# One matmul stream cut into small pieces: convolution and transposes interleaved on TensorE, with seven landing slots ahead of it

## What is computed

```python
x = x + conv3x3_int8(group_norm(x, 16 groups), weight, bias)   # per-tensor scales: max|.| over all of x
x = x + spectral(group_norm(x, 16 groups), R)                  # rfft2, keep 32 x 16 modes, mix channels, irfft2
```

## Time and profile before

| | |
|---|---|
| time, median of 3 runs (range) | 3774.03 us (3768.83 to 3782.59) |
| the profiled execution's own time, and its span | 3779.11 us, 3777.3 us |
| mean granted clock of TensorE | 0.909 |
| first stage, about 10 to 765 us | VectorE 576 of 715 us busy, DMA 362 GB/s |
| second stage, 790 to 2427 us | TensorE 1567, VectorE 1542, ScalarE 1360 of 1637 us busy, DMA 328 GB/s |
| last stage, 2515 to 3777 us | VectorE 1061 of 1262 us busy, DMA 419 GB/s |

### The profile page before, as it was taken

How to read it: one execution, slowest core, us unless ns; L and a number is a source line. 1 busy time by engine, 2 the same in 40 slices (tenths; PEclk the granted TensorE clock), 3 DMA queues, 4 the chain that set the end, 5 groups by cost and what they waited for, 6 DMA issues and landing times.

```text
span 3777.3 us, 81588 instructions
## 1 busy us (share of the span) xinstructions
PE 3106.2 (82%) x33145; PEld 1541.2 (41%) x33145; DVE 3256.8 (86%) x3336; ACT 2350.9 (62%) x3443; POOL 823.0 (22%) x1040
## 2 busy tenths in 40 slices
PE   5565566569999999999999999878888888888886
PEld 1111111136666666666666666543222222222222
DVE  5878878799999998999999998669888888888887
ACT  5777777768888787878888888643333333333332
POOL 0000000035455454545455454300000000000000
PEclk7767666689999999999999999989999999999998
DMA  9999999999999999999999999749999999999998
GB/s 359 366 359 356 357 361 365 357 250 356 336 319 347 306 354 295 352 306 345 324 332 334 317 346 301 279 170 427 427 427 427 427 427 427 427 423 422 421 421 370
DMA packets 342540, 1352.55 MB, mean 358 GB/s; under 512 B 45792, under 2 KB 47040, under 8 KB 243808
## 3 DMA queue, kind: packets, MB, share of 16 engines
q1 hardware_dynamic: 223104, 811.13, 60.0%
q0 software_dynamic: 82272, 268.58, 19.8%
q10 hardware_dynamic: 36864, 268.45, 16.9%
HBM read 811.10 MB, written 536.87 MB: 357 GB/s over the span
## 4 chain that ended last, share of the span: by engine, by line
DMA 39%; DVE 34%; PE 14%; issue 6%; ACT 5%; SPq 1%; POOL 0%; DVEq 0%; ACTq 0%
DMA out<-ring 19%; DVE ring L561 12%; DMA ring<-in_x 11%; DMA ring<-x_scratch 9%; DVE area L543 6%; ACT area L312 4%; PE ps L721 4%; DVE area L538 4%; PE ps L683 4%; DVE area L547 3%; DVE ring L658 3%; PE ps L732 2%; DVE area L556 2%; PE ps L742 1%; DVE mixb L566 1%
## 5 line engine op out<-in xcount | busy, mean ns | idle before, releaser
L288 POOL DMA_DIRECT2D x_scratch<-ring x1024 | 817.0, 804 | 1596.9 <-DVE ring L561 1574.1
L868 PE MATMUL ps<-x,gj_s 128*128 128x512 bf16 x3072 | 773.6, 406 | 217.2 <-DVE ring L658 216.2
L721 PE MATMUL ps<-area,wq 128*32 128x512 bf16 x12264 | 764.8, 383 | 51.0 <-DVE ring L561 33.7
L658 DVE TENSOR_TENSOR ring<-ps,ring 128x1024 f32<-128x1024 f32 x512 | 603.0, 1219 | 162.5 <-DMA ring<-x_scratch 159.2
L561 DVE SCALAR_TENSOR_TENSOR ring<-ps,sc,ring 128x1024 f32<-128x1024 f32 x512 | 634.2, 1278 | 19.7 <-PE ps L721 12.6
L683 PE MATMUL ps<-ring,negm_s 128*32 128x512 f32 x2048 | 391.4, 905 | 313.4 <-DMA ring<-in_x 313.4
L337 ACT ACTIVATE area<-ps 128x512 f32<-128x512 f32 x1024 | 553.2, 595 | 116.2 <-PE ps L732 115.2
L868 PEld LDWEIGHTS ps<-x,gj_s 128*128 128x128 bf16 x3072 | 294.8, 103 | 773.9 <-DVE ring L658 442.8
L732 PE MATMUL ps<-id_s,ring 128*128 128x128 f32 x4096 | 561.3, 280 | 16.2 <-ACT area L337 14.1
L466 DVE TENSOR_REDUCE stat<-area 128x1 f32<-128x4096 f32 x128 | 559.1, 4410 | 7.1 <-ACT area L312 7.0
L344 ACT ACTIVATE area<-ring,qtab 128x2048 bf16<-128x2048 f32 x256 | 513.1, 2004 | 0.0
(11 more groups left out here) (123 smaller groups left out, 2006.3 us busy)
## 6 DMA issues: line engine op xcount, KB each, us to landing
ring<-in_x SPq DMA_DIRECT2D x256, 1024.0 KB, 7.9
ring<-in_x SPq DMA_DIRECT2D x1024, 256.0 KB, 6.9
x_scratch<-ring POOLq DMA_DIRECT2D x1024, 256.0 KB, 6.6
ring<-x_scratch SPq DMA_DIRECT2D x256, 1024.0 KB, 11.7
out<-ring ACTq DMA_DIRECT2D x256, 1024.0 KB, 25.3
ring<-in_rt SPq DMA_DIRECT2D x1, 4096.0 KB, 15.2
area<-in_gj SPq DMA_DIRECT2D x1, 768.0 KB, 4.7
eh_s<-in_eh SPq DMA_DIRECT2D x1, 128.0 KB, 2.0
```

The costliest lines, as they stand in the source:

```text
L288: pool.dma_start(x1_rows[b, m, r], xslot(t % SL)[32 * r:32 * r + 32, :].rearrange("p (g w) -> p g w", g=4)).then_inc(s_x_out[t % SL], 16)
L658: nc.vector.tensor_tensor(half, ps[0][:, hj * 2 * HW:(hj + 1) * 2 * HW], half, ALU.add).then_inc(s_add, 1)
L721: last = mm(ps[0][32 * cg:32 * cg + 32, HW * g:HW * g + HW], wq[:, (3 * a + dw) * C:(3 * a + dw + 1) * C], src[:, 1 + dw:1 + dw + HW], sta ...
L868: last = mm(bank(j), gj_s[:, (j * 3 + v) * 128:(j * 3 + v + 1) * 128], (z12, z12, z13)[v][:, k % 2], start=(v == 0), stop=(v == 2))
```

## The change

Three things are changed, all in the first two stages.

The first stage gets seven landing slots in place of four; slots 4 to 6 are the buffers `vbuf`, `mixb` and `x2`, which only later stages use. The first loads of the second stage wait for the last group that used their slot.

`rows_copied` moves from VectorE to ScalarE, in two places of its loop, and the rest of the small work of an image is put later: the copy of the height transform from j = 5 to 6, `dc_first` from 6 to 7, `sums` from 6 to 8, `spread` from 7 to 9, `variance` from 7 to 11, `root` from 8 to 12, `spectra` from 9 to 12, `spectrum` from 9 to 14. The loops run to T + 20 instead of T + 15.

On TensorE, `conv` and `turn_x1` are cut into a group of four matmuls (one g and dw) and a single transpose. `conv_and_turn(i-2, i-4, h)` issues six groups of four, and behind each of them one transpose, behind the third and the sixth two. The same instructions are issued as before, in another order, with the same semaphores.

```diff
+        NGS = 7
+
         def gslot(k):
-            return ring[:, k * FT:(k + 1) * FT]
+            return ring[:, k * FT:(k + 1) * FT] if k < 4 else (vbuf, mixb, x2)[k - 4][:, 0:FT]
...
-                if n >= 4:
-                    sp.wait_ge(s_sq, n - 3)
+                if n >= NGS:
+                    sp.wait_ge(s_sq, n - NGS + 1)
                 for c in range(GC):
-                    sp.dma_start(gslot(n % 4)[:, c * FC:(c + 1) * FC], x_chan[GC * n + c]).then_inc(s_g_in[n % 4], 16)
+                    sp.dma_start(gslot(n % NGS)[:, c * FC:(c + 1) * FC],
+                                 x_chan[GC * n + c]).then_inc(s_g_in[n % NGS], 16)
...
-                    sp.wait_ge(s_sq, NT - 3 + t // 2)
+                    sp.wait_ge(s_sq, max(n for n in range(NT) if n % NGS == t // 2) + 1)
                 load(t)
...
+            def rows_copied(b, n):
+                act.wait_ge(s_vt, 8 * b + n + 1)
+                act.activation(vt[:, :, 4 * n:4 * n + 4, :],
+                               bank(7).rearrange("p (c g k) -> p g c k", c=4, g=8), ACT.Copy).then_inc(s_vte, 1)
...
-            for i in range(T + 15):
+            for i in range(T + 20):
                 b, j = divmod(i - (TB + 5), TB)
                 small = i >= TB + 5
                 if i + 1 < T:
                     scaled(i + 1)
                 if 6 <= i and i - 6 < T and (i - 6) % 4 == 3:
                     w_copied(i - 6)
-                if small and j == 5:
+                if small and j == 6:
                     h_copied(b)
+                if small and 1 <= j < 5:
+                    rows_copied(b, 2 * j - 1)
                 if 4 <= i and i - 4 < T:
                     turned(i - 4, 0)
                     turned(i - 4, 1)
                     squared(i - 4)
+                if small and j < 4:
+                    rows_copied(b, 2 * j)
+                if 4 <= i and i - 4 < T:
                     turned(i - 4, 2)
                     turned(i - 4, 3)
-                if small and j == 8:
+                if small and j == 12:
                     root(b)
...
-            def rows_copied(b, n):
-                dve.wait_ge(s_vt, 8 * b + n + 1)
-                nc.vector.tensor_copy(vt[:, :, 4 * n:4 * n + 4, :],
-                                      bank(7).rearrange("p (c g k) -> p g c k", c=4, g=8)).then_inc(s_vte, 1)
...
-            for i in range(T + 15):
+            for i in range(T + 20):
                 b, j = divmod(i - (TB + 5), TB)
                 small = i >= TB + 5
                 if 3 <= i and i - 3 < T:
                     combine(i - 3, 0)
                     combine(i - 3, 1)
-                if small and 1 <= j < 5:
-                    rows_copied(b, 2 * j - 1)
                 if i < T:
                     quantise(i)
                 if i == T:
                     nc.vector.memset(qs[64:128, 15, :], 0.0).then_inc(s_q, 1)
-                if small and j < 4:
-                    rows_copied(b, 2 * j)
-                if small and j == 6:
+                if small and j == 8:
                     sums(b)
-                if small and j == 7:
+                if small and j == 11:
                     variance(b)
-                if small and j == 9:
+                if small and j == 14:
                     spectrum(b)
 
...
-            def conv(t, h):
-                if h == 0:
+            def conv_group(t, g, dw):
+                if dw == 0 and g == 0:
                     pe.wait_ge(s_q, t + 2)
-                if t:
-                    pe.wait_ge(s_ev, 2 * (t - 1) + h + 1)
-                for g in (2 * h, 2 * h + 1):
-                    n = 4 * (t % 4) + g
-                    above = qs[:, n - 1] if n else (qs[:, 15] if t % TB else qedge)
-                    for dw in range(3):
-                        for cg, a, src in ((1, 0, q[:, n]), (2, 1, q[:, n]), (3, 0, qs[:, n]), (0, 1, above)):
-                            last = mm(ps[0][32 * cg:32 * cg + 32, HW * g:HW * g + HW],
-                                      wq[:, (3 * a + dw) * C:(3 * a + dw + 1) * C], src[:, 1 + dw:1 + dw + HW],
-                                      start=(dw == 0), stop=(dw == 2))
-                last.then_inc(s_conv, 1)
-
-            def turn_x1(t, v):
-                if v == 0:
-                    pe.wait_ge(s_ev, 2 * t + 2)
-                if 4 * t + v >= 2:
-                    pe.wait_ge(s_te, 4 * t + v - 1)
-                for g in range(4):
-                    last = nc.tensor.transpose(bank(4 + v % 2)[:, 128 * g:128 * g + 128],
-                                               xslot(t % SL)[:, g * HW + 128 * v:g * HW + 128 * v + 128], id_s[:])
-                last.then_inc(s_t, 1)
+                if t and dw == 0 and g % 2 == 0:
+                    pe.wait_ge(s_ev, 2 * (t - 1) + g // 2 + 1)
+                n = 4 * (t % 4) + g
+                above = qs[:, n - 1] if n else (qs[:, 15] if t % TB else qedge)
+                for cg, a, src in ((1, 0, q[:, n]), (2, 1, q[:, n]), (3, 0, qs[:, n]), (0, 1, above)):
+                    last = mm(ps[0][32 * cg:32 * cg + 32, HW * g:HW * g + HW],
+                              wq[:, (3 * a + dw) * C:(3 * a + dw + 1) * C], src[:, 1 + dw:1 + dw + HW],
+                              start=(dw == 0), stop=(dw == 2))
+                if dw == 2 and g % 2:
+                    last.then_inc(s_conv, 1)
+
+            def turn_x1(t, v, g):
+                if g == 0:
+                    if v == 0:
+                        pe.wait_ge(s_ev, 2 * t + 2)
+                    if 4 * t + v >= 2:
+                        pe.wait_ge(s_te, 4 * t + v - 1)
+                last = nc.tensor.transpose(bank(4 + v % 2)[:, 128 * g:128 * g + 128],
+                                           xslot(t % SL)[:, g * HW + 128 * v:g * HW + 128 * v + 128], id_s[:])
+                if g == 3:
+                    last.then_inc(s_t, 1)
+
+            def conv_and_turn(tc, tt, h):
+                turns = [(2 * h + v, g) for v in range(2) for g in range(4)]
+                for k in range(6):
+                    if 0 <= tc < T:
+                        conv_group(tc, 2 * h + k // 3, k % 3)
+                    if 0 <= tt < T:
+                        for v, g in turns[(0, 1, 2, 4, 5, 6)[k]:(1, 2, 4, 5, 6, 8)[k]]:
+                            turn_x1(tt, v, g)
...
-            for i in range(T + 15):
+            for i in range(T + 20):
                 b, j = divmod(i - (TB + 5), TB)
                 small = i >= TB + 5
-                if 4 <= i and i - 4 < T:
-                    turn_x1(i - 4, 0)
-                    turn_x1(i - 4, 1)
-                if 2 <= i and i - 2 < T:
-                    conv(i - 2, 0)
+                conv_and_turn(i - 2, i - 4, 0)
                 if small and j < 4:
                     turn_rows(b, 2 * j)
-                if 4 <= i and i - 4 < T:
-                    turn_x1(i - 4, 2)
-                    turn_x1(i - 4, 3)
-                if 2 <= i and i - 2 < T:
-                    conv(i - 2, 1)
+                conv_and_turn(i - 2, i - 4, 1)
                 if 5 <= i and i - 5 < T:
                     along_w1(i - 5)
                 if small and j < 4:
                     turn_rows(b, 2 * j + 1)
                 if small and j == 4:
                     along_h1(b)
-                if small and j == 6:
+                if small and j == 7:
                     dc_first(b)
-                if small and j == 7:
+                if small and j == 9:
                     spread(b)
-                if small and j == 9:
+                if small and j == 12:
                     spectra(b)
```

More of the change, by code:

```diff
@@ L151, in build @@
         s_rl = sem("r_landed")
-        s_g_in = [sem(f"group_landed{k}") for k in range(4)]
+        s_g_in = [sem(f"group_landed{k}") for k in range(NGS)]
         s_cols = sem("group_column_sums_done")
@@ L311, in squares @@
                     act.wait_ge(s_max, n - 1)
-                act.activation(sqs[:, n % 2], gslot(n % 4), ACT.Square, bias=st(1, n),
+                act.activation(sqs[:, n % 2], gslot(n % NGS), ACT.Square, bias=st(1, n),
                                accum_out=st(2, n)).then_inc(s_sq, 1)
@@ L677, in column_sums @@
             def column_sums(n):
-                pe.wait_ge(s_g_in[n % 4], (n // 4 + 1) * 32)
+                pe.wait_ge(s_g_in[n % NGS], (n // NGS + 1) * 32)
                 if n >= 4:
@@ L682, in column_sums @@
                     g = j % 4
-                    last = mm(bank(n % 4)[32 * g:32 * g + 32, :], negm_s[:], gslot(n % 4)[:, j * HW:(j + 1) * HW],
+                    last = mm(bank(n % 4)[32 * g:32 * g + 32, :], negm_s[:], gslot(n % NGS)[:, j * HW:(j + 1) * HW],
                               start=(j < 4), stop=(j >= 4))
```

## The result

The changed kernel takes 4288.29 us (median of 4 runs, 4286.45 to 4292.53) against 3778.31 us of the kernel before on the same chip (3768.83 to 3788.16, 4 runs). The ratio is 1.135, 95% interval 1.132 to 1.138: 510 us slower. The forecast was 4300 us, range 4160 to 4440. The profiled execution took 4289.36 us, its span is 4287.5.

The account below looks back on a forecast made before the run. VectorE was taken to bound the second stage at 5.93 us a chunk, and TensorE at 8.50 after interleaving. 3779 + 626 (second stage) - 98 (slots) = 4307 us profiled; median 4302, say 4300, range 4160 to 4440.

Parts of the forecast that it names:

- the price of a border: Second stage, TensorE: each round trip from convolution to transposes and back costs 0.275 us; twelve make a chunk 8.50 us.
- The bet: Second stage, TensorE: a border costs the same around a single transpose as around a run, giving 8.50 us a chunk.
- 626 us longer: Second stage: 255 chunks of 8.50 us plus 84 us of small work make 2252 us, against 1626 before.
- The small work of an image: Second stage, TensorE as the bound: its own small work costs 84 us over seven images, 12 us each.
- The copies on ScalarE: Second stage: rows_copied moved off VectorE is covered in a chunk of 8.50 us, costing nothing and bringing nothing.
- Seven slots: First stage: DMA rises from 362 to 419 GB/s and binds; 124 groups save 0.79 us each, 98 us.
- the rules weighed in the forecast: TensorE: a tiling mode change drains it (8.50 us a chunk), or weight loads are pulled ahead (5.2 us).
- The rival in which everything hides: Second stage: transposes' weights load beneath the convolution, no border paid, VectorE binds at 5.93 us; 3596 us, chance 0.06.
- The break-even of that rival: Second stage: the hidden-loads rival decides at a chunk of about 6.4 us, or 0.10 us a round trip.
- the later places of the small work: Second stage: the later j are covered, VectorE's waits for TensorE's small matmuls being no longer on the path.
- The clock's rival: Second stage: TensorE's clock falls to 0.94, a chunk takes 8.9 us and the kernel 4410 us; chance 0.07.
- One reading of a row: Last stage: TensorE stands idle over a microsecond in each 4.9, its clock at 0.94.

Follow-up runs that it names:

- e4: Changed kernel with two groups of four between transposes, which come three, three and two together, six round trips a chunk instead of twelve: 3892.95 us, ratio 1.029.
- e9: Changed kernel, still interleaved, each group of four 128 x 32 matmuls made one with 128 x 128 weights (convolution computes other values): 3632.2 us, ratio 0.961.
- e11: Changed kernel with the copies of turned rows back on VectorE, small work still late: 4288.63 us, ratio 1.134.
- e1: Changed kernel with only TensorE's order undone, eight transposes of a half ahead of its six groups: 3656.3 us, ratio 0.966 against the kernel before.
- e12: Changed kernel with TensorE's block order restored and part of its small work left out (height transform 1 of 4 steps, spectra 1 of 16): 3601.55 us, ratio 0.952.
- e10: Changed kernel with the small work of an image at its old, early places, copies still on ScalarE: 4424.21 us, ratio 1.170.
- e3: Kernel before with TensorE's interleaving alone (four slots, copies on VectorE, small work at its old place): 4530.52 us, ratio 1.197.
- e5: Changed kernel, interleaved, each transpose replaced by four identity matmuls with 32 columns of the chunk as weights: 4409.24 us, ratio 1.167.
- e6: Changed kernel with each transpose replaced by four 32-column identity matmuls, in the block order of the kernel before: 4315.98 us, ratio 1.143.

## Why the prediction was right, and where it was not

The step that carries it, the price of a border read from the kernel before, held to a few per cent. I took 0.275 us for a round trip and 8.50 us a chunk; measured are 0.27 and 8.41. The bet was that a border costs a single transpose as much as a run of eight, for which the trace before had no row; e4 and the changed kernel show it at both lengths. The streams (0.216, 0.108) are unchanged, and e9 shows a chunk interleaved without its borders. The stage was forecast 626 us longer and became 611 longer.

The small work of an image was put at 12 us on TensorE. The stage has 2236.5 - 255 x 8.41 = 92 us left, 13 for each of seven ends; some 5 of the 92 stand at the stage's start, where the clock is at 0.50 from 700 to 725 us, so an end costs the 12. The copies on ScalarE were forecast to be covered: e11, 4288.63 us, shows them worth nothing.

Seven slots were forecast at 98 us, with DMA at 419 GB/s: 103 us and 421 GB/s in the trace.

Of the rules weighed in the forecast: where TensorE changes from 32-column to 128-column weights it waits, 0.33 us between starts, of which 0.216 stream. The Trainium skill's page "TensorEngine Tiling (Array Packing)", Key Properties, says that a change of tiling mode drains TensorE, and the trace agrees. Weight loads are pulled ahead too, 0.21 us in e9, but in these traces only within one shape. The Trainium skill's page "TensorE: Matmul & The Clock Gate", Step-by-step, says that loads can be pulled ahead of matmuls in flight; for the changes of shape here that did not happen.

Two statements of the forecast were wrong, neither of them a term of its sum. The rival in which everything hides was priced at 3596 us, with 11 of 16 us of each image's end saved. e1 is that state of the path and takes 3656 us: the ends cost 14 us, because I counted VectorE's waits and copies as gains and overlooked that TensorE, at 5.75 of 5.93 us, has no room for its own 12. e12 shows it. The break-even of that rival moves with it, and the chance doesn't.

And the later places of the small work I called covered, with no worth of their own. In the changed kernel they are covered, but they do something: at their old places they would have added 136 us (e10): VectorE waits ahead of its combines, TensorE then waits 48 us for these, and the clock at 1.2 GHz behind the waits costs about 90 more. A forecast of the interleaving alone by the same steps would have come out at 4385 us, with 4530 measured (e3).

The clock's rival didn't come: 0.99 over the stage. e10 shows how near it was. There the clock falls to the 0.94 that the forecast named, a chunk takes 13.8 us at half clock where it said some 14, and the kernel 4424 us where it said 4410. The forecast weighed the rival by TensorE's short pauses between groups and had no reason why the image ends would be free of longer ones. That the late places kept them free was luck.

One reading of a row was off: in the last stage TensorE stands idle (1262 - 1032.54)/256 = 0.90 us for each channel image by its records, not over a microsecond. No term hangs on it.

## What to carry to other kernels

Read TensorE from the starts of its records, not from its busy time: 2224 of 2226 us were "busy" here, and over a third of a chunk (12 x 0.27 of 8.41 us) was borders. Work of two weight shapes belongs in long runs, at 0.27 us for each round trip between 32 and 128 columns; if it must be interleaved, give both the same shape, and then weight loads hide as well. When one engine is made slower, look at what waits at the end of its turn: a small matmul there holds up the engine that should feed it next, and the pause can cost more through the clock than by its length (90 and 48 us in e10). The version to keep is e1, seven slots, the copies on ScalarE and the later small work with TensorE's order left in blocks, 3.4% faster than the kernel before.

## What the runs showed of the hardware that was not expected

The supply of instructions seems able to bound TensorE. e5 and e6 had gaps of up to 5.0 and 3.6 us between the starts of their records, mostly multiples of 256 instructions apart, 191 to 214 us in 1200, when a chunk of 7 us of streams had 208 matmul records and as many weight loads. In the changed kernel, with half as many, the same stretch has 5 gaps over 0.45 us, 2.6 us in all. What in the supply is the limit stays open; no run varies it.

The price of a border was nearly the same at the lower clock. At 1.2 GHz, in e10, a group and its transpose take 1096.47 - 1095.51 = 0.96 us. If the streams take twice their time at 2.4 GHz, 0.43 and 0.22, 0.31 us are left for the round trip, against 0.27 at 2.4 GHz. This is an estimate from one stretch.
